# Scaling z's rows on GpSimd in place of VectorE in the count stage of a graph and feed-forward kernel

## The reference, cut to what matters

```python
z = jnp.einsum('ni,hoi->hno', h, W)             # 4 heads of 64 columns
e = e_src[:, src] + e_dst[:, dst]
e = jnp.where(e > 0, e, NEG_SLOPE * e)          # NEG_SLOPE = 0.01
ex = jnp.exp(e_h - m[dst])
den = segment_sum(ex, dst)
out = segment_sum((ex / den[dst])[:, None] * z_h[src], dst)
```

## Time and profile before

| | |
|---|---|
| median of 3 runs | 1695.35 us (1694.79 to 1695.71) |
| the profiled execution's own time | 1694.51 us |
| its span, first to last instruction | 1692.8 us |
| mean granted TensorE clock | 0.98 of full |
| the count stage | 70 to 263 us of the span |

### The profile page before, as it was taken

The page is one execution under the profiler, slowest core; times in us unless marked ns, Lnnn a source line. Parts: engine busy times, 40 slices in busy tenths (PEclk is TensorE's granted clock), DMA queues, the critical chain, the costliest instruction groups (busy, mean ns, idle before and its releaser), DMA issues. The chain is left out here.

```text
span 1692.8 us, 33810 instructions
## 1 busy us (share of the span) xinstructions
PE 1547.1 (91%) x11582; PEld 1354.6 (80%) x11582; DVE 1031.5 (61%) x1831; ACT 1030.3 (61%) x1884; POOL 82.6 (5%) x117
## 2 busy tenths in 40 slices
PE   5788886999999999989998999999999999999696
PEld 4577766999999999966665999977799998776465
DVE  6799995899999999974454221132421222876661
ACT  2566675888889898853433656556565555566220
POOL 3000000000000000020000100000000000120213
PEclk9899998999999999989999999999999999999799
DMA  7335640644736555027660545445454444666211
GB/s 215 98 92 142 155 118 29 158 109 96 157 74 136 107 104 112 1 70 145 142 139 9 127 111 127 114 127 133 129 141 119 125 109 117 162 151 154 65 48 39
DMA packets 236969, 190.60 MB, mean 113 GB/s; under 512 B 107274, under 2 KB 231624, under 8 KB 236848
## 3 DMA queue, kind: packets, MB, share of 16 engines
q1 hardware_dynamic: 226938, 176.22, 43.4%
q0 software_dynamic: 6368, 9.36, 2.2%
q10 hardware_dynamic: 3542, 3.46, 0.8%
HBM read 114.58 MB, written 53.86 MB: 100 GB/s over the span
## 5 line engine op out<-in xcount | busy, mean ns | idle before, releaser
L1662 PE MATMUL ps_sets<-arena,kinds_mem 125*125 125x195 bf16 (+1 forms) x2500 | 445.7, 250 | 28.3 <-DVE kinds_mem L1403 18.6
L1387 ACT ACTIVATE kinds_mem<-ed_rows,es_mask 125x625 bf16<-125x625 f32 x500 | 366.5, 809 | 61.7 <-PE ps_sets L1668 34.0
L1668 PE MATMUL ps_sets<-arena,kinds_mem 125*125 125x195 bf16 (+1 forms) x2300 | 394.8, 249 | 0.0
L1662 PEld LDWEIGHTS ps_sets<-arena,kinds_mem 125*125 125x125 bf16 x2500 | 343.1, 137 | 36.4 <-DVE kinds_mem L1403 25.6
L2863 ACT ACTIVATE onewide<-ring 125x625 fp32r (+1 forms) x325 | 222.5, 720 | 168.6 <-PE oneps L2580 95.3
L1668 PEld LDWEIGHTS ps_sets<-arena,kinds_mem 125*125 125x125 bf16 x2300 | 315.5, 137 | 0.0
L2552 PE MATMUL oneps<-onewide,parts_a 125*128 125x376 f32 (+1 forms) x2000 | 293.0, 308 | 8.0 <-DVEq L2643 8.0
L2552 PEld LDWEIGHTS oneps<-onewide,parts_a 125*128 125x128 f32 x2000 | 291.2, 190 | 8.9 <-DVEq L2641 8.4
L2580 PE MATMUL oneps<-oneparts_b,onewide 125*125 125x512 f32 x1000 | 234.6, 395 | 0.0
L2580 PEld LDWEIGHTS oneps<-oneparts_b,onewide 125*125 125x125 f32 x1000 | 184.5, 185 | 48.6 <-DVE onefull L2715 1.9
L1395 DVE TENSOR_TENSOR kinds_mem<-kinds_mem,blk 125x2500 bf16<-125x2500 bf16 x120 | 182.3, 1520 | 40.5 <-ACT kinds_mem L1387 31.4
(11 more groups left out here) (447 smaller groups left out, 1823.9 us busy)
## 6 DMA issues: line engine op xcount, KB each, us to landing
ring<-counts SPq DMA_DIRECT2D x50, 683.6 KB
ring<-countsT SPq DMA_DIRECT2D x40, 683.6 KB
countsT<-cut_mem SPq DMA_DIRECT2D x107, 136.7 KB
blk<-counts SPq DMA_DIRECT2D x20, 546.9 KB
counts<-blk SPq DMA_DIRECT2D x3, 3418.0 KB
counts<-kinds_mem SPq DMA_DIRECT2D x2, 3418.0 KB
ed_rows<-ed_dram SPq DMA_DIRECT2D x16, 273.4 KB
ring<-countsT SPq DMA_DIRECT2D x10, 410.2 KB
```

Of the source, the lines that this page charges most:

```text
L1387: return k.nc.scalar.activation(kinds_of(k)[:, slot, 0, :], k.ed_b[:, h, :], ACT.Relu, scale=MASK_SCALE, bias=k.es_mask[:, t, h:h + 1])
L1662: t_.matmul(out[0], kind[0], z[0], start=(t == 0), stop=False)
L1668: last = t_.matmul(out[1], kind[1], z[1], start=False, stop=(t == T - 1))
```

## The change

scale(t) moves from VectorE's program to GpSimd's, with the same operands. There it stands behind L728 and the clearing of semaphores: scale(0) and scale(1) follow exps_done, the others wait for the same two semaphores as before. VectorE no longer waits for exps_done; in front of the padding memset its drain is replaced by a wait for all 25 scales. TensorE's, ScalarE's and SP's programs stay as they are.

```diff
--- before.py
+++ after.py
@@ -729,6 +729,23 @@
                 nc.gpsimd.drain().then_inc(eye_set, 1)
                 clear_past(k, pool)
 
+                def scale(t):
+
+                    if not isinstance(t, int):
+
+                        pool.wait_ge(part_done[0], t - 1)
+                        pool.wait_ge(rest_done[1], t - 1)
+                    nc.gpsimd.tensor_tensor(out=full(t), in0=zs[:, bass.ds(t, 1), :].rearrange("p a (h c) -> p (a h) c", h=HEADS)[:, :, 2:Z1].unsqueeze(2)
+                                            .to_broadcast([P, HEADS, 2, D1]),
+                                            in1=src_exp[:, bass.ds(t, 1), :, :].rearrange("p a h e -> p (a h) e").unsqueeze(3)
+                                            .to_broadcast([P, HEADS, 2, D1]), op=ALU.mult).then_inc(scaled, 1)
+
+                pool.wait_ge(exps_done, 1)
+                scale(0)
+                scale(1)
+                with pool.Fori(2, T) as t:
+                    scale(t)
+
             @block.vector
             def _(dve):
                 top_b = k.top[:, :].unsqueeze(1).to_broadcast([P, T, HEADS])
@@ -747,36 +764,20 @@
                 v.tensor_tensor(out=k.dst_exp[:, :, :, 1], in0=k.dst_exp[:, :, :, 1], in1=m_dst[:, :, :], op=ALU.subtract)
                 v.drain().then_inc(terms_done, 1)
 
-                def scale(t):
-
-                    if not isinstance(t, int):
-
-                        dve.wait_ge(part_done[0], t - 1)
-                        dve.wait_ge(rest_done[1], t - 1)
-                    v.tensor_tensor(out=full(t), in0=zs[:, bass.ds(t, 1), :].rearrange("p a (h c) -> p (a h) c", h=HEADS)[:, :, 2:Z1].unsqueeze(2)
-                                    .to_broadcast([P, HEADS, 2, D1]),
-                                    in1=src_exp[:, bass.ds(t, 1), :, :].rearrange("p a h e -> p (a h) e").unsqueeze(3)
-                                    .to_broadcast([P, HEADS, 2, D1]), op=ALU.mult).then_inc(scaled, 1)
-
                 def hots(i, first):
                     for u in range(U):
                         if not first:
 
                             dve.wait_ge(hist_done, U * (i - 1) + u + 1)
-                        if u == 1:
-                            if first:
-                                dve.wait_ge(exps_done, 1)
-                            scale(i)
                         v.tensor_tensor(out=hot[:, u, :, :, :, :].rearrange("q g e r c -> q (g e) r c"), in0=k.iota_rep[:, :, :, :],
                                         in1=k.cutG[:, bass.ds(i * U + u, 1), :, :, :].rearrange("q a g e c -> q (a g e) c").unsqueeze(2)
                                         .to_broadcast([128, 2 * U, P, 2]), op=ALU.is_equal).then_inc(hot_done, 1)
 
                 hots(0, True)
-                hots(1, False)
-                with dve.Fori(2, T) as i:
+                with dve.Fori(1, T) as i:
                     hots(i, False)
 
-                v.drain()
+                dve.wait_ge(scaled, T)
                 v.memset(zrows(k)[:, :, 0, :, W3:WP].rearrange("p t e a -> p t (e a)"), 1.0)
                 dve.wait_ge(blk_done, U * T + U)
                 for m in range(EARLY):
```

## The result

| | kernel before | changed kernel |
|---|---|---|
| median | 1695.53 us (1694.79 to 1698.9, 4 runs) | 1709.66 us (1708.4 to 1710.03, 4 runs) |
| the profiled execution | 1694.51 us, span 1692.8 | 1709.81 us, span 1708.1 |
| first comparison to first product of the next stage | 271.68 - 70.21 = 201.5 us | 285.85 - 72.27 = 213.6 us |

A forecast was written before the change was run, and what follows sets the result against it. VectorE was taken to bound the count stage, tied at 7.467 us a tile with a 7.44 us loop. 25 x (1.23 - 0.61) = +15.5, less 1.0 absorbed, gave +14.5 us: 1709.8 us, range 1700 to 1725.

The forecast's parts named there:

- the hold: Count stage: each GpSimd scale holds VectorE's comparisons off, 1.23 us a tile in place of 0.61 us of removed work.
- the stop: Early in the stage GpSimd gets no turn until VectorE fills its five buffers; forecast only as starving, up to 6.85 us.
- second rival: Count stage: GpSimd gets in only where VectorE stops for a free buffer; some +21.5 us, 1716.8 us; chance 0.13.
- VectorE sets the pace, tied with a second loop at 7.44 us: Count stage: VectorE takes 7.467 us a tile, TensorE and ScalarE's loop 7.44; relieving VectorE gains at most 1.3 us.
- GpSimd's product takes 1.27 us: Each 125x520 fp32 scale on GpSimd: 0.186 us fixed plus 2.09 ns an element; bounds 0.62 and 1.68 us.
- Each scale costs VectorE the whole GpSimd instruction: Beside the comparisons: 1.27 - 0.12 + 0.09 = 1.23 us a scale, against 0.61 removed; +15.5 us over 25 scales.
- 1.0 us is absorbed at the end: At the stage's last histogram, 2.66 us behind its comparison against 1.66 in mid-stage: 1.0 us of the delay is absorbed.
- The row at 762.39 as the case against: VectorE products pass a one-tensor GpSimd operation unheld; supports the first rival, no holding off, 1694.0 us, chance 0.15.
- Signs named beforehand: Count stage: comparisons of some 2.7 us, scales 8.1 us apart, VectorE never idle, TensorE's L770 wait some 30 us.

The follow-up runs named there:

- the later timing: The changed kernel, unedited, timed again beside the kernel before: 1707.36 us, ratio 1.0065.
- the three kernels with a shortened loop: Third z part early on the kernel before: 1694.24 us; GpSimd writing ones instead of the product, on the changed kernel: 1693.54 us; both together: 1681.74 us.
- the experiment with the stop removed: Changed kernel with VectorE waiting for scale(i) in front of the second comparison of tile i: 1704.03 us, ratio 1.0046; timed again, 1703.52 us, ratio 1.0044.
- the memsets: Changed kernel with GpSimd writing ones into full(t) in place of the product, its later scales written out: 1693.54 us, ratio 0.9976.

## Why the prediction was right, point by point

The forecast of 1709.8 us was met by 1709.66, and that closeness is luck. The mechanism that it chose, the hold, is there and makes the kernel slower, but it is only half of the loss: it was sized at more than double, and the rest came from the stop, which the prediction had as its second rival. The two errors offset each other. The stage lost 6.3 us by the holds and 5.8 us by the stop, 12.1 in all, where the forecast had 14.5 by holds alone; the last 2 us between the medians are the scatter outside the stage. In the later timing the medians are only 11.15 us apart (1696.21 and 1707.36).

*VectorE sets the pace, tied with a second loop at 7.44 us.* Right in kind: shown by the three kernels with a shortened loop. Mis-sized by 0.07 us: the second loop is 7.37 us, so "at most 1.3 us" was 2.9.

*GpSimd's product takes 1.27 us.* Too high: it is 1.056 us when VectorE stands still, (1.056 - 0.186) / 520 = 1.67 ns an element in place of 2.09. The row of 20 partitions and 256 elements was the nearest one, not a near one.

*Each scale costs VectorE the whole GpSimd instruction.* Right, but **this is the term that was mis-sized: 1.23 us, measured 0.87** (2.31 - 1.45). (The prediction's own terms, 1.27 - 0.12 + 0.09, make 1.24; that slip is 0.25 us of its sum.) Besides the shorter product, 0.19 us of it pass while it waits, not 0.12, and no overlap is lost: the comparison behind a long one starts 1.37 + 0.87 us after it. The term is 25 x (0.865 - 0.61) = 6.4 us where the forecast had 15.5; the experiment with the stop removed shows 6.3, with 24 holds and a wait of 1.1 us in it.

*GpSimd starves* was the second rival, with 0.13. It did happen, once in a stage instead of every ten tiles, and costs 5.8 us; the rival's 1717 us had longer holds in it and up to 6.85 us of starving. Its mechanism was told rightly (TensorE at the rest product, ScalarE at L814, five full buffers), but when it sets in was not: it goes not by VectorE's lead, but with the number of comparisons since GpSimd's last turn.

*1.0 us is absorbed at the end.* It was 0.2: VectorE's stretch from first to last comparison grew by (269.84 - 72.27) - (255.47 - 70.21) = 12.3 us, the stage by 12.1. VectorE's own sum closes: 23 holds x 0.865 = 19.9, less 25 x 0.61 = 15.3, and 7.6 us of stop, 12.2 us.

*The row at 762.39 as the case against.* Rightly read as a difference between one-tensor and two-tensor operations on GpSimd; the rule of the Trainium skill ("SBUF — State Buffer", Who interferes with whom) that any GpSimd instruction that reads SBUF contends with a VectorE instruction with two SBUF inputs is borne out both ways for the two-tensor product. For the one-tensor operation the runs bear it out one way only: it is held off (0.448 to 3.0 us), but the comparisons beside it take 1.55 us at most. The same section says that a GpSimd instruction which only writes doesn't contend with such a VectorE instruction; the trace agrees, with comparisons of 1.464 us at most beside the memsets.

*Signs named beforehand.* Long comparisons: 2.31 in place of the 2.7 us named. Tile 7.71 in place of 8.1. "No idle time on VectorE" was wrong, 7.6 us in one piece, and it was the sign that I had given for the second rival. TensorE's wait for the comparisons did not grow (14.8 us): its idle time grew before the rest products instead, from 23.8 to 31.9 us, the stop among it. The group in the kernel before:

```profile
L868 PE MATMUL ps_rest<-head_sums,ident 125*125 (+1 forms) x200 | 62.7, 401 | 23.8 <-issue 22.4 <-ACT arena L817 1.4
```

## What to carry to other kernels

In these runs VectorE's comparisons (two SBUF inputs) and GpSimd's two-input product ran one after the other, so work moved from one to the other in such a loop pays only if its hold is shorter than the work taken off VectorE; here 0.87 us of hold replaced 0.61 us of work. An engine busy all the time is worth relieving only as far as the next loop: walk that loop first, 7.37 against 7.47 us here left 2.9 us to win. A GpSimd instruction beside a gapless row of such VectorE instructions should come often, or VectorE should wait for it at a place where it is usually done; here that wait brought back 5.8 of the 12.1 us.

## What the runs showed of the hardware that was not expected

GpSimd's turn goes with the number of comparisons since its last one: in 163 cases with at most four it got in at the next boundary or at once, in all 6 cases with six or seven it got in only when VectorE stopped, 8 to 13 us later. No case fell on five while VectorE ran on, and the count was varied on purpose only once. It is at the same time the number of comparisons that VectorE had run in a row since it was last held or stopped, and the runs don't tell these two apart; what in the chip makes the difference stays open.

A one-tensor GpSimd operation of 65 columns (0.448 us alone, up to 3.0 us beside comparisons) is held off by VectorE's two-input comparisons and delays them by some 0.1 us at most, where the two-tensor product delays them by 0.87 us.
